# Attention key weights of batches 3 to 15 formed for groups of batches and kept in DRAM

## What is computed

```python
q = x @ Wq.T                       # Wq: 1024 x 256, 16 heads of 64
k, v = split(context @ Wkv.T)      # context: 16 x 64 x 256
sim = einsum('bhid,bhjd->bhij', q, k) * 64 ** -0.5
out = softmax(sim) applied to v, then @ Wout.T + b_out
x = layernorm(x + out)
```

## Time and profile before

| | |
|---|---|
| three runs | 1277.95 us median (1277.67 to 1278.22) |
| the profiled execution's own time | 1278.95 us |
| its span | 1277.2 us |
| busy in the span: TensorE, DVE, ScalarE, GpSimd | 97%, 69%, 45%, 50% |
| 0 to 73 us | setup |
| 73 to 117 us | iterations -2 and -1 |
| 117 to about 917 us | 16 batches of attention |
| to the end | experts |

### The profile page before, as it was taken

The page is one execution under the profiler, slowest core; times in us unless marked ns, Lnnn a source line. Parts: engine busy times, 40 slices in busy tenths (PEclk is TensorE's granted clock), DMA queues, the critical chain, the costliest instruction groups (busy, mean ns, idle before and its releaser), DMA issues.

```text
span 1277.2 us, 22575 instructions
## 1 busy us (share of the span) xinstructions
PE 1240.4 (97%) x8080; PEld 1123.7 (88%) x8080; DVE 874.9 (69%) x1696; ACT 570.2 (45%) x1119; POOL 632.2 (50%) x986
## 2 busy tenths in 40 slices
PE   8968999999999999999999999998999999999998
PEld 7857999999999999999999999887798899899888
DVE  5536988888889888888888898887534323323335
ACT  2124546555555465555655554654524313412420
POOL 3215756767667567576675675665422112112201
PEclk9979999999999999999999999999999999999999
DMA  9831111011111021111111111140140111011001
GB/s 278 200 74 34 35 34 54 26 55 43 34 50 51 26 59 34 43 42 35 51 49 34 51 42 34 39 124 22 34 132 14 55 66 67 1 67 67 1 1 34
DMA packets 117475, 69.98 MB, mean 55 GB/s; under 512 B 74099, under 2 KB 114804, under 8 KB 117365
## 3 DMA queue, kind: packets, MB, share of 16 engines
q1 hardware_dynamic: 115332, 67.87, 18.2%
q10 hardware_dynamic: 2032, 0.66, 0.2%
HBM read 42.29 MB, written 26.22 MB: 54 GB/s over the span
## 4 chain that ended last, share of the span: by engine, by line
PE 87%; DVE 4%; POOL 1%; issue 1%; ACT 1%; POOLq 0%; DVEq 0%
PE ob L137 7%; PE ob L138 7%; PE ob L139 7%; PE sim L137 7%; PE sim L138 7%; PE sim L139 7%; PE pw L417 4%; PE pt L466 4%; PE pw L137 3%; PE pw L138 3%; PE pw L139 3%; PE pw L369 3%; PE pt L138 2%; PE pt L139 2%; PE pt L137 2%; PE pw L393 2%
## 5 line engine op out<-in xcount | busy, mean ns | idle before, releaser
L1513 POOL TENSOR_TENSOR w_lo<-w_raw,w_hi 128x2048 fp32r<-128x2048 f32 x16 | 73.8, 4614 | 222.7 <-ACT w_hi L1453 169.6
L137 PE MATMUL ob<-b_hi,pT_hi 128*128 128x256 f32 x512 | 153.0, 299 | 3.8 <-DVE pT_lo L822 3.8
L139 PE MATMUL ob<-b_hi,pT_lo 128*128 128x256 f32 x512 | 144.7, 283 | 0.0
L138 PE MATMUL ob<-b_lo,pT_hi 128*128 128x256 f32 x512 | 144.6, 282 | 0.0
L902 POOL TENSOR_TENSOR prob<-prob,rz 128x512 f32<-128x512 f32 x128 | 131.1, 1045 | 11.5 <-DVE rz L769 11.5
L684 ACT ACTIVATE prob<-prob 128x512 f32<-128x512 f32 x128 | 80.8, 632 | 112.5 <-DVE prob L815 111.7
L810 DVE TENSOR_REDUCE mx<-sim 128x8 f32<-128x512 f32 x128 | 87.9, 687 | 37.4 <-PE sim L139 36.1
L596 ACT ACTIVATE x<-h,nmr,rstd 128x256 f32<-128x256 f32 x128 | 76.3, 596 | 64.2 <-POOL nmr L836 59.2
L137 PEld LDWEIGHTS ob<-b_hi,pT_hi 128*128 128x128 f32 x512 | 97.3, 190 | 8.5 <-DVE pT_lo L822 7.8
L137 PE MATMUL sim<-a_hi,tT_hi 128*128 128x512 f32 x256 | 104.2, 407 | 0.0
L829 POOL TENSOR_SCALAR ve<-mv 128x1 f32<-128x1 f32 x128 | 28.1, 219 | 148.9 <-DVE mv L732 147.5
(11 more groups left out here) (241 smaller groups left out, 3871.6 us busy)
## 6 DMA issues: line engine op xcount, KB each, us to landing
xraw<-in_x SPq DMA_DIRECT2D x16, 512.0 KB, 4.0
kv_scratch<-stage SPq DMA_DIRECT2D x32, 256.0 KB, 2.8
x_scratch<-x SPq DMA_DIRECT2D x64, 128.0 KB, 1.7
out_x<-o_sb SPq DMA_DIRECT2D x64, 128.0 KB, 1.7
w_raw<-in_L_ffn_experts_inter SPq DMA_DIRECT2D x8, 1024.0 KB, 5.0
w_raw<-in_L_ffn_experts_out SPq DMA_DIRECT2D x8, 1024.0 KB, 7.7
kraw<-kv_scratch SPq DMA_DIRECT2D x32, 128.0 KB, 2.9
vraw<-kv_scratch SPq DMA_DIRECT2D x32, 128.0 KB, 3.1
```

What stands on the lines that cost most here:

```text
L137: pe.matmul(out, lh, rh, start=first, stop=False)
L138: pe.matmul(out, lh, rl, start=False, stop=False)
L139: return pe.matmul(out, ll, rh, start=False, stop=last)
```

## The change

Batches 0, 1 and 2 keep the old way: their A pieces are now A0 to A3 (batch 0), C0 to C3 (batch 1) and D0 to D3 (batch 2), all made in iterations -2 and -1. C and D are copied by ScalarE alone and stored to `a_scratch` in DRAM (`store_rows`, in pieces of 112, 15 and 128 partitions, since partition 0 of the first half holds the mask row).

For batches 3 to 8 and 9 to 15, sixteen units (eight pairs of heads for each group) are made in slots 0 to 31. A unit loads the keys of one pair for all batches of its group twice one above the other (`k_twice`, 384 or 448 columns) and 64 rows of the weights in the same way (`w_twice`). ScalarE rounds both (`act_stack`), GpSimd subtracts (`pool_stack`), so that a 128-row contraction of which only 64 are distinct holds high and low part together. TensorE makes four pieces U?0 to U?3 of two fp32r matmuls each instead of eight of plain fp32 records for four blocks; ScalarE copies a piece into `a_stage`, and SP stores it in three DMAs for each unit (`store_unit`).

In slot 3 of each batch SP loads A of the next batch from `a_scratch` straight into `a_lo`, in two halves, each once `sim` of tile 3 has read the old half; ScalarE rounds it to `a_hi` (128x2x512), DVE subtracts in place. `sim` of slot 0 waits for `a_ready`, half by half. Fifteen mask rows go to DRAM in setup by 15 DMAs more, the keys lie in `k_scratch` as rows of 2 KB for each partition. `ORDER` is a new table for all preps, and on ScalarE, DVE and GpSimd some steps of a slot trade places.

```diff
@@ setup_and_attention
+    OLD = 3
+    GROUPS = (slice(OLD, 9), slice(9, NB))
+    UNIT_SLOTS = (0, 1, 3, 4, 5, 7, 8, 9, 12, 15, 16, 19, 20, 23, 27, 31)
+    STACK_SLOTS = (0, 1, 2, 4, 5, 6, 8, 9, 12, 13, 16, 17, 20, 21, 25, 29)
...
@@ ORDER
-        "A1": ((3, 1), (3, 0), (3, 2)), "A0": ((3, 1), (3, 1), (3, 3)),
...
+        "U31": ((2, 9), (2, 19), (3, 3)), "U30": ((3, 1), (3, 1), (3, 3)),
...
@@ sp_slot
+        if early_pieces(n):
+            store_unit(sp, n, 0)
+        if slot == 3 and it >= 0 and within(it + 1):
+            for h in range(2):
+                sp.wait_ge(s["sim_made"], 2 * n + h + 1)
...
+                sp.dma_start(f32(half(a_lo, h)), a_scr[it + 1, :, :, h * HK:(h + 1) * HK]).then_inc(s[f"a_loaded{h}"], 16)
...
+        for u in stacked_in(n):
+            if u + 1 < 2 * PAIRS:
+                sp.wait_ge(s["stack_made"], u + 1)
+                load_unit(sp, u + 1)
...
@@ pe_prep
+            pe.wait_ge(s["stack_made"], u + 1)
+            c = slice(m * P, (m + 1) * P)
+            pe.matmul(pw[:, g], w_stack_hi[:, e, c], k_stack[:, e, g], start=True, stop=False)
+            last = pe.matmul(pw[:, g], w_stack_lo[:, e, c], k_stack[:, e, g], start=False, stop=True)
...
@@ pe_sim
-                prep_done(pe, it - 1, last_of("A0", "A1"))
-                need(pe, "mask_in_a", 16 * (it + 1))
...
+            pe.wait_ge(s["a_ready"], 2 * (it - 1) + h + 1)
...
+    def act_stack(act, u):
+        act.wait_ge(s["r_loaded"], 32 * (u + 1))
...
+        act.activation(k_stack[:, :, g], k_twice[:, :, g], ACT.Copy)
+        act.wait_ge(s["w_loaded"], 32 * (u + 1))
+        act.activation(w_stack_hi[:, :, :], w_twice[:, :, :], ACT.Copy).then_inc(s["stack_hi"], 1)
+    def act_a(act, b, h):
+        act.wait_ge(s[f"a_loaded{h}"], 16 * b)
+        act.activation(half(a_hi, h), f32(half(a_lo, h)), ACT.Copy).then_inc(s["a_hi_made"], 1)
...
+    def dve_a(dve, b, h):
+        dve.wait_ge(s["a_hi_made"], 2 * (b - 1) + h + 1)
+        dve.tensor_tensor(half(a_lo, h), f32(half(a_lo, h)), f32(half(a_hi, h)), ALU.subtract).then_inc(s["a_ready"], 1)
...
+    def pool_stack(pool, u):
+        pool.wait_ge(s["stack_hi"], u + 1)
+        lo, g = slice(64, P), slice(0, (batches_of(u).stop - batches_of(u).start) * NKV)
+        pool.tensor_tensor(w_stack_lo[:, :, :], w_twice[:, :, :], f32(w_stack_hi[:, :, :]), ALU.subtract
+                           ).then_inc(s["w_lo_made"], 1)
+        pool.wait_ge(s["w_lo_made"], u + 1)
+        pool.tensor_tensor(k_stack[lo, :, g], k_twice[lo, :, g], f32(k_stack[lo, :, g]), ALU.subtract
+                           ).then_inc(s["stack_made"], 1)
```

More of the change, by code:

```diff
@@ L186, in setup_and_attention, with unit_of, batches_of, pieces_of @@
     sbdT = k.sb("sbdT", [P, MC, P])
+    OLD = 3
+    GROUPS = (slice(OLD, 9), slice(9, NB))
+    GK = max(g.stop - g.start for g in GROUPS) * NKV
+    UNIT_SLOTS = (0, 1, 3, 4, 5, 7, 8, 9, 12, 15, 16, 19, 20, 23, 27, 31)
+    STACK_SLOTS = (0, 1, 2, 4, 5, 6, 8, 9, 12, 13, 16, 17, 20, 21, 25, 29)
+    UNITS = {n: u for u, n in enumerate(UNIT_SLOTS)}
+    assert len(UNITS) == 2 * PAIRS
+    k_stack = k.sb_over("wqx", "k_stack", [P, 2, GK])
+    w_stack_hi = k.sb_at("w_stack_hi", [P, 2, C], F32R, k.offsets["wqx"] + 8 * GK)
+    w_stack_lo = k.sb_at("w_stack_lo", [P, 2, C], F32R, k.offsets["wqx"] + 8 * GK + 8 * C)
+    k_twice = k.sb_over("kraw", "k_twice", [P, 2, GK], F32)
+    a_stage = k.sb_over("w2_raw", "a_stage", [P, MC, GK // NKV, 2, NKV], F32)
+    w_twice = k.sb_at("w_twice", [P, 2, C], F32, first.w1_at + 8 * FF - 8 * C)
+    a1_stage = k.sb_over("w2_raw", "a1_stage", [P, 2, MC, HK], F32)
+    def unit_of(it, name):
+        return UNITS[TPB * it + int(name[1])]
+    def batches_of(u):
+        return GROUPS[u // PAIRS]
+    def pieces_of(n):
+        return [f"U{n % TPB}{j}" for j in range(4)]
+    STORES = (2, 1)
+    def early_pieces(n):
+        return n in UNITS and n % TPB == 3
+    def stacked_in(n):
+        return [u for u, m in enumerate(STACK_SLOTS) if n == m]
     zw_hi = k.sb("zw_hi", [P, 6, P], F32R)
@@ L529, in pe_slot @@
         prep(3)
+        if tail_tile(it, slot) is not None:
+            ff["pe_up"](pe, 0, tail_tile(it, slot))
+        prep(4)
         if has_x1T or has_xT:
             pe_tr(pe, n, it + 2, slot, par(1 if slot else 0), par(0), has_x1T, has_xT)
-        prep(4)
+        if has_z:
+            pe_z(pe, it, slot)
+        prep(6)
         if (it, slot) == (NB - 1, 1):
@@ L550, in pe_slot @@
             ff["pe_transposes"](pe, 0, 0)
+        prep(11)
         if (it, slot) == (NB - 1, 1):
             ff["pe_transposes"](pe, 0, 3)
-        if tail_tile(it, slot) is not None:
-            ff["pe_up"](pe, 0, tail_tile(it, slot) + 1)
+        prep(12)
         if has_prev:
             pe_pB(pe, n - 1, it if slot else it - 1, (slot - 1) % 4, 1)
-        prep(8)
+        prep(13)
     def prep_views(name):
@@ L678, in act_slot @@
             ff["act_weights"](act, 0, 0, 0, 3)
+        prep(17)
+        if loads_a(it, slot):
+            act_a(act, it + 1, 1)
+        prep(18)
         if slot == STATE_SLOT and has_state(it):
             act_sums(act, it)
+        prep(19)
+        if (it, slot) == (NB - 1, 2):
+            ff["act_small"](act)
     def act_exp(act, n, q, h):
@@ L751, in dve_slot @@
             dve_max(dve, n, 0)
-        prep(2)
         if has_sim:
@@ L802, in dve_slot @@
             dve_stats(dve, 1, n + 4, q, h1[:, q, :])
+        if (it, slot) == (NB - 1, 3):
+            ff["dve_small"](dve)
+        prep(17)
+        if loads_a(it, slot):
+            dve_a(dve, it + 1, 1)
+        if tail_tile(it, slot) is not None:
+            ff["dve_up"](dve, 0, tail_tile(it, slot) + 1)
+        prep(19)
     def by_head(ap):
@@ L903, in pool_slot @@
                                    ALU.mult).then_inc(s["p_ready"], 1)
+        if slot == 3 and within(it + 1):
+            need(pool, "v_hi_made", it + 2)
+            pool.tensor_tensor(v_lo[:, :, :], vraw[:, :, :], f32(v_hi[:, :, :]), ALU.subtract).then_inc(s["v_lo_made"], 1)
+        if tile_exists(n + 5):
+            pool_xb(pool, n + 5, it + 1 if slot < 3 else it + 2, (slot + 1) % 4, par(1 if slot < 3 else 2))
         if has_z:
@@ L912, in pool_slot @@
             ff["pool_small"](pool)
-        if (it, slot) == (NB - 1, 0):
-            ff["pool_weights"](pool, 0, 0, 0)
-    FIRST_PREPS = [n for n in NAMES if enabled(n, -2) and n[0] != "Q"]
+    FIRST_PREPS = [n for n in NAMES if enabled(n, -2) and n[0] not in "AQ"]
     def first_prep(eng, kind, i):
```

278 lines of the change are left out of this document (188 added, 90 removed), and 26 rows, old and new, of the table ORDER.

## The result

The changed kernel takes 1297.44 us (median of 4 runs, 1296.20 to 1302.23) against 1278.09 us of the kernel before (4 runs, 1277.67 to 1278.78): ratio 1.0156, 95% interval 1.0145 to 1.0168. It is 19 us slower, 31 above the forecast and outside its range. The profiled execution's span is 1294.6 us (before 1277.2).

What follows compares the result with a forecast made beforehand. The prediction took TensorE (97% busy, 87% of the chain) as the bound, until DVE stops it. Terms -29.5 + 7.8 + 1 + 2.5 + 5 + 1 = -12.2 us gave 1266 us; range 1253 to 1283, forecast case 1259 to 1271 (chance 0.5).

Steps and rivals of the forecast that it cites:

- the border of two batches: Slot 3 into slot 0: DVE's second subtraction ends at about 12.5 us, TensorE asks at 13.3; cost 0.
- DVE and GpSimd hold each other: Rival, slot 3: `a_lo` subtractions and GpSimd's `prob`, `v_lo` block each other; 18 +-5 us at 15 borders, about 1276; chance 0.2.
- the DVE term: Batches 8 to 13: DVE's limit takes back 1.3 us a batch, +7.8 us in all (0 to +15.6).
- The half load is late: Rival, slot 3: a half of A landing beyond about 10.5 us stops TensorE at slot 0, 15 times; 1288; chance 0.1.
- TensorE's sum in the loop: Batch loop: A preps of 15 sets go, -53.4 us; matmuls of 16 units come, +23.9; together -29.5 us.
- DVE in the loop: Batch loop: DVE stays at about 43.5 us a batch; batches 8 to 13 take 48.3 us each, +7.8 in all.
- The 49.6: Batches 8 to 13: upper end of a batch's time in us, if DVE sets the pace as at the end of attention.
- The first eight batches: Batches 0 to 7: win next to nothing, 404 us against 400; DVE's limit adds +1 (0 to +2).
- Work I count at nothing: ScalarE's copies (some 3.4 us a unit), GpSimd's subtractions (3 us a unit) and SP's loads have room; cost 0.
- wrong in any case: Sign: unit batches above 53 us would mean that ScalarE or GpSimd was not free.
- Setup and iterations -2 and -1: Before the loop: mask DMAs and `kraw` loads +1 us (0 to +3); moved A, C, D preps +5 (0 to +12).
- The end of attention: Slot 3 of batch 14: of 3.56 us of A preps about 1 is won, +2.5 against the sum (0 to +3.6).

Runs made afterwards that it cites:

- low_one_input: The changed kernel with both DVE subtractions of `a_lo` replaced by a maximum over `a_hi` (1024 columns, one SBUF operand); 1273.26 us, ratio 0.9962.
- low_cut: The changed kernel with DVE's subtractions of `a_lo` cut to 8 columns of each row block; 1270.48 us, ratio 0.9946.
- loads_first: The changed kernel with both half loads of A put ahead of the unit's stores in SP's slot 3; 1298.34 us, ratio 1.0162.
- v_lo_first: The changed kernel with GpSimd's `v_lo` of slot 3 moved ahead of the wait for DVE's statistics; 1281.69 us, ratio 1.0022.
- the best version: The changed kernel with `v_lo` moved ahead, half loads before unit stores, and the first half's rounded part also in the `sim` banks; 1269.66 us, ratio 0.9939.
- the two clearer pairs of runs: `v_lo_first` and `low_one_input`, each without and with GpSimd's unit subtractions cut to 8 columns: 1281.69 and 1277.82 us; 1273.26 and 1271.50 us.
- stack_cut: The changed kernel with GpSimd's two subtractions of a unit cut to 8 columns (the first unit's `w_stack_lo` whole); 1292.85 us, ratio 1.0125.

## Why the prediction was wrong

**The step that failed** is "the border of two batches", with its "So it fits by 0.8 us: 0", and the chance given to the rival *DVE and GpSimd hold each other*. The border was counted with 1.2 us for a subtraction; they took 2.01 on average and up to 3.3. The rest of that count was right. In the border shown above, slot 0 starts on TensorE 10.5 us after slot 3 (counted 10.5), DVE's second subtraction is issued after 11.8 (11.3), and TensorE asks for it after 13.45 (13.3). With 1.2 us it would have ended at 13.0 and fitted; with 2.77 it ended at 14.6. That rival named the place, the partners (`prob` and `v_lo`) and the signs (`a_lo` over 1.2 us, `prob` and `v_lo` longer), and had 0.2. The Trainium skill (SBUF — State Buffer, Who interferes with whom) states that a DVE instruction with two SBUF inputs contends with a GpSimd instruction that reads SBUF, and that the order of issue decides which of the two blocks. The trace agrees on every point: 2.77 us beside `v_lo`, 1.2 alone, 684 ns and no effect on GpSimd with one operand in PSUM. No row of the kernel before showed it, but the instruction's form did, and I weighed the lack of a row as doubt.

**Its price** was too small as well. I took 18 us (13 to 23) for 15 borders, and set 8 of them against the DVE term. Measured, the whole time falls by 24 (`low_one_input`) and 27 us (`low_cut`); in batches 0 to 14, where the borders lie, by 19.5 and 24.5, or 1.3 to 1.6 a border. Nothing was to be set off: in batches 8 to 13 TensorE waits 1.3 us for `a_lo` and, at another place, 0.4 for `pT_lo`, and with the hold gone the 0.4 stays and they take 47.7.

**The half load is late** is the rival in whose range (1282 to 1300) the result fell, and both its signs were there: 20.5 us of waits before `sim`, and ScalarE waiting 10.2 us for the load. It is still not what made the changed kernel slow: with the loads in time (`loads_first`) the time is the same, and with the hold gone and the loads as late as before (`low_one_input`, ScalarE waiting 11.4 us for them) it is 24 us less. It was real in seven batches with units: there the first half landed 5.8 to 6.8 us after its issue against 4.1 to 4.2 in the others, by the bytes before it, as the prediction said, and SP issued it late besides, behind a store that waits for ScalarE. The two together are worth 0 in the changed kernel, 7 to 11 us once `v_lo` stands first.

**TensorE's sum in the loop** held in its prices: four matmuls of a unit's two pieces take 0.81 us between starts (422.89 to 423.70 in the timeline of `v_lo_first`), 0.20 each as worked out for 448 columns. Its busy time is 0.5 to 1.1 us a batch above the sum; part of that goes with the pauses (47.5 in the changed kernel, 47.3 in the best version). **DVE in the loop**: 48.3 was taken for batches 8 to 13, 47.7 is right without the hold, 49.2 with it. The 49.6, from DVE at 88%, came close to 49.2 for a wrong reason.

**The first eight batches** were 23.7 us off. 13 of them are the hold by `low_cut` (421.5 to 408.3); by `low_one_input`, 8. Of the 10.5 left in `low_cut`, 7 lie in batches 1 to 7. There I applied a rule wrongly: I let DVE's limit count only where TensorE's sum is smaller. In fact TensorE waits 0.4 to 0.5 us for `pT_lo` in each of these batches too, as in those without units, and is busy 0.5 to 0.8 us above the sum, for which no run shows the reason. The other 3 are batch 0 (51.3 us, before 47.6), with three units right after the first `sim`: beside the 0.7 us for `b_lo` that was there before, TensorE waits 0.5 each for ScalarE's `x` and for `k_stack` and 0.4 for `pT_lo`, and it is busy 1 us above the sum. (These waits are from TensorE's timeline of `low_cut`.)

**Errors that cancel.** Without the hold (`low_cut`) the span is 2.8 us above the forecast's. That looks like a good sum and is in part luck: batches 0 to 7 are 10.5 over it, batches 8 to 13 3.2 under it, and the time to the first `sim` 4.1 under it.

**Work I count at nothing**: GpSimd's stack, 2 to 4 us by the two clearer pairs of runs (0 to 8 by `stack_cut`). Four unit batches came out above 53 us, the sign named as "wrong in any case"; its "ScalarE or GpSimd was not free" is true of GpSimd in that it was held and, for the smaller part, by the stack. **Setup and iterations -2 and -1** were 3 us cheaper together than taken, which is within what runs differ by there. **The end of attention** won nothing with the hold and 1.7 us without it (44.3 to 42.6, forecast 43.2).

## What to carry to other kernels

Before an operand is moved from PSUM to SBUF, look at what GpSimd runs at that time: here a DVE instruction with two SBUF operands cost, beside its own time, what the GpSimd instruction that it met had left, and delayed the one after, on a border that had no slack for it. Such a hold shows as longer instructions and not as idle time, so compare the mean of a group, and min to max of one tile, with the same form elsewhere. Causes that stand in one wait hide each other: the order on SP was worth nothing alone and 7 us behind another edit, so try the second cause again after the first is gone. And a waiting time before an instruction doesn't name its cause: here the late load left both its signs and was worth nothing until the hold was gone.

## What the runs showed of the hardware

A DVE subtraction of 16 columns a partition with both operands in SBUF took up to 2095 ns beside GpSimd, with a minimum of 257; the one shown above ended with GpSimd's `v_lo`. So the hold can be many times as long as the held instruction. Even GpSimd's 128x1 `ve` is held (1.10 us at 643.30 above, normally 0.22). A reduction over 1024 columns from SBUF, in the same place, varied by 37 ns in all.
